# Graph attention kernel, layer 1: the tile's running sum added inside PSUM by an identity matmul and copied back by ScalarE

## What is computed

```python
h = (x @ W).reshape(n, NHEAD, OUT_FEATS)
h_l = (a_l * h).sum(-1)
h_r = (a_r * h).sum(-1)
e = h_l[row] + h_r[col]
e = jnp.where(e > 0, e, ALPHA * e)
m = jax.ops.segment_max(e, row, num_segments=n)
ex = jnp.exp(e - m[row])
denom = jax.ops.segment_sum(ex, row, num_segments=n)
att = ex / (denom[row] + 1e-16)
msg = att[:, :, None] * h[col]
out = jax.ops.segment_sum(msg, row, num_segments=n)
```

## Time and profile before

| | |
|---|---|
| median of 3 runs | 2378.44 us (2374.66 to 2379.36) |
| the profiled execution | 2369.76 us |
| its span (first to last instruction) | 2368.0 us |
| PE busy in the span | 1942.9 us, 82% |
| DVE busy | 1809.6 us, 76% |
| ACT busy | 1484.2 us, 63% |
| POOL busy | 1480.6 us, 63% |
| mean granted clock of PE | 0.939 |

### The profile page before, as it was taken

The page is one execution under the profiler, slowest core; times in us unless marked ns, Lnnn a source line. Parts: engine busy times, 40 slices in busy tenths (PEclk is TensorE's granted clock), DMA queues, the critical chain, the costliest instruction groups (busy, mean ns, idle before and its releaser), DMA issues.

```text
span 2368.0 us, 44546 instructions
## 1 busy us (share of the span) xinstructions
PE 1942.9 (82%) x9766; PEld 1418.9 (60%) x9767; DVE 1809.6 (76%) x4313; ACT 1484.2 (63%) x5321; POOL 1480.6 (63%) x1468
## 2 busy tenths in 40 slices
PE   0889999999938988889898999856777787878774
PEld 0457777777726777777776777633444454545442
DVE  7873333333339998999999999785999998999987
ACT  2236666666637777777777777447666666666660
POOL 3737777777777666666666656137666666666660
PEclk9999999999969999999999999986998988898997
DMA  8343333333339888988888885024344333333311
GB/s 239 123 183 133 131 130 132 131 130 132 122 135 328 292 298 292 299 289 300 301 290 301 303 286 169 3 69 132 102 109 107 107 103 102 107 108 101 107 36 54
DMA packets 162160, 403.34 MB, mean 170 GB/s; under 512 B 46887, under 2 KB 59099, under 8 KB 162108
## 3 DMA queue, kind: packets, MB, share of 16 engines
q0 software_dynamic: 79360, 276.09, 36.1%
q1 hardware_dynamic: 82748, 126.67, 17.0%
HBM read 343.89 MB, written 84.72 MB: 181 GB/s over the span
## 4 chain that ended last, share of the span: by engine, by line
PE 31%; DVE 29%; issue 16%; DMA 9%; POOL 6%; DVEq 4%; ACT 3%; SPq 0%; ACTq 0%; POOLq 0%
PE ps L1449 12%; DMA arena<-sorted_edges 6%; DVE gmx L1291 5%; POOL sorted_edges L573 4%; PE ps L1435 4%; PE ps L1482 3%; PE ps L1485 3%; DVE arena L1323 3%; DVE sc L1134 2%; PE ps L1497 2%; DVE arena L1120 2%; DVE work L1286 2%; DVEq L337 2%; PE ps L1607 2%; DVE arena L1127 2%
## 5 line engine op out<-in xcount | busy, mean ns | idle before, releaser
L642 POOL DMA_INDIRECT arena<-node_row,idxC x464 | 485.5, 1046 | 234.4 <-issue 133.1
L573 POOL DMA_INDIRECT sorted_edges<-work,idxA x416 | 404.9, 973 | 145.8 <-issue 143.1
L1091 DVE TENSOR_TENSOR work<-ps,b_bc 128x512 f32<-128x512 f32 x208 | 143.8, 691 | 322.2 <-PE ps L1449 322.2
L1449 PE MATMUL ps<-w_sb,arena 128*128 128x256 f32 x1664 | 386.7, 386 | 0.0
L1607 PE MATMUL ps<-arena,hq 128*128 128x260 f32 x928 | 281.6, 431 | 91.6 <-DVE work L1286 88.1
L1449 PEld LDWEIGHTS ps<-w_sb,arena 128*128 128x128 f32 x1664 | 307.7, 190 | 71.8 <-issue 33.8
L597 POOL DMA_INDIRECT work<-node_kvx,idxB x232 | 247.0, 1065 | 147.9 <-issue 50.9
L597 POOL DMA_INDIRECT arena<-node_kvx,idxB x232 | 246.0, 1060 | 146.1 <-issue 56.0
L712 ACT ACTIVATE work<-work 128x256 f32<-128x256 f32 x416 | 188.7, 500 | 194.1 <-DVE work L1091 194.0
L1291 DVE TENSOR_REDUCE gmx<-ps 128x4 f32<-128x1024 f32 x232 | 282.8, 1219 | 28.7 <-PE ps L1582 28.6
L1482 PE MATMUL ps<-arena,work 128*128 128x256 f32 x928 | 254.8, 398 | 57.9 <-issue 37.6
(11 more groups left out here) (206 smaller groups left out, 3858.7 us busy)
## 6 DMA issues: line engine op xcount, KB each, us to landing
arena<-sorted_edges SPq DMA_DIRECT2D x232, 260.0 KB, 4.7
work<-sorted_rows SPq DMA_DIRECT2D x58, 256.0 KB, 3.6
arena<-in_edge_attr SPq DMA_DIRECT2D x25, 512.0 KB
node_kvx<-arena SPq DMA_DIRECT2D x24, 384.0 KB, 2.3
arena<-node_row,idxC POOLq DMA_INDIRECT x464, 3.3
sorted_edges<-work,idxA POOLq DMA_INDIRECT x416, 2.4
sorted_edges<-arena SPq DMA_DIRECT2D x25, 260.0 KB
sorted_edges<-arena SPq DMA_DIRECT2D x1, 6240.0 KB
```

Of the source, the lines that this page charges most:

```text
L573: pool.indirect_dma_start(rec_dram[:, :], bass.IndirectOffsetOnAxis(ap=idxA[:, st.slot(8), c:c + 1], axis=0), recA[:, st.slot(8), c, :], N ...
L642: pool.indirect_dma_start(row1_g[:, st.slot(16), j, :], None, row1_dram[:, :], bass.IndirectOffsetOnAxis(ap=idxC[:, batch(st).slot(4), st. ...
L1449: ins = pe.matmul(ps[:, 5 + t, half * H:(half + 1) * H], hidT[:, r, m, half, t * P:(t + 1) * P], w2_sb[:, m, :], start=m == 0, stop=m == 1)
```

## The change

The sum of a tile no longer passes through DVE.

- **PE**: after the two one-hot matmuls of a step (now 15 steps behind, L1616 of the changed kernel), a third f32 matmul, identity times the tile's `acc1`, adds the old sum in the same bank (L1623). It waits for `acc1_done` of the step before, or, in the first step of a batch, for `acc1_scaled`. Its operand's address is a register, so PE now reads the table `gt_i` every eight steps, between the L1601 matmuls and the one-hot matmuls.
- **ACT**: a copy of the bank to `acc1` (L862), 17 steps behind, placed after `indices`, `pen` and `onehT1` and ahead of the copy of `hrT`. It has a table read of its own every eight steps. The one-hot matrices are made four steps later than before; the exponentials stand at the fourth step of a batch, one step earlier.
- **DVE**: the add is gone. The scale by `mscale` stays, once per batch, now behind the maximum (L1299), and waits for `acc1_done` of the step before. Both table reads of a turn stand behind the maximum.
- `msg1` becomes a ring of eight, half of it in `hq` behind the one-hot matrices; a new semaphore `msg1_used` frees its slots and those of `oneh1`. The table gets 32 columns in front where it had 16, and `ended` shares memory with `away`.

```diff
@@ scalar, layer1
+                if st.u % 8 == 0:
+                    act_tiles[17] = tiles16(ACT_ENGINE, st.k, 17, st.u // 8)
+                d = st.back(17)
+                if d.real():
+                    act.wait_ge(s("agg1_ready"), d.n + 1)
+                    act.copy(acc1[:, bass.ds(act_tiles[17][st.u % 8], 1), :].rearrange("p a n -> p (a n)"),
+                             agg1[d.slot(2)]).then_inc(s("acc1_done"), 1)
...
-                if st.real():
-                    act.wait_ge(s("srcC_ready"), b.n + 1)
+                h = st.back(4)
+                if h.real():
+                    act.wait_ge(s("srcC_ready"), batch(h).n + 1)
...
-                e = b.back(3)
-                if g == 0 and e.real():
+                e = b.back(2)
+                if g == 3 and e.real():
@@ vector, layer1
-                    dve.wait_ge(s("agg1_ready"), c.n + 1)
-                    dve.tensor_tensor(acc, acc, agg1[c.slot(2)], ALU.add).then_inc(
-                        s("acc1_done"), 1)
...
+                if st.u % 8 == 0:
+                    tiles[11] = tiles16(DVE, st.k, 11, st.u // 8)
+                c = st.back(11)
+                if c.real() and c.u % BG == 0:
+                    acc, k = tile(acc1, tiles[11][st.u % 8]), batch(c)
+                    dve.wait_ge(s("mscale"), k.n + 1)
+                    if not c.first(1):
+                        dve.wait_ge(s("acc1_done"), c.n)
...
-                    if not m.first(2):
-                        dve.wait_ge(s("agg1_ready"), m.n - 1)
+                    if not m.first(8):
+                        dve.wait_ge(s("msg1_used"), m.n - 7)
@@ tensor, layer1
-                d = st.back(13)
+                if st.u % 8 == 0:
+                    pe_tiles[15] = tiles16(PE, st.k, 15, st.u // 8)
+                d = st.back(15)
...
+                        ins = pe.matmul(agg1[r], oneh1[:, r16, j, :], msg1(d)[:, j, :],
+                                        start=j == 0, stop=False)
+                    ins.then_inc(s("msg1_used"), 1)
+                    if d.u % BG == 0:
+                        pe.wait_ge(s("acc1_scaled"), batch(d).n + 1)
+                    else:
+                        pe.wait_ge(s("acc1_done"), n)
+                    pe.matmul(agg1[r], ident[:, :],
+                              acc1[:, bass.ds(pe_tiles[15][st.u % 8], 1), :].rearrange("p a n -> p (a n)"),
+                              start=False, stop=True).then_inc(s("agg1_ready"), 1)
```

More of the change, by code:

```diff
@@ L38 @@
 AHEAD = 2
+FRONT = 32
 class Step:
@@ L279, in gnn_kernel @@
         away = sb("away", [P, 2, GJ, P])
+        ended = away.rearrange("p r c n -> p (r c n)")[:, 0:NG]
         sc = sb("sc", [P, 2, GJ, NH0])
@@ L330, in tiles_of @@
             _, values = nc.values_load_multi_w_load_instructions(
-                gt_i[0:1, bass.ds(k * 8 + (16 - lag), count)], engines=(eng,), min_val=0, max_val=NT - 1,
+                gt_i[0:1, bass.ds(k * 8 + (FRONT - lag), count)], engines=(eng,), min_val=0, max_val=NT - 1,
                 skip_runtime_bounds_check_because="the table's values are bounded by the minimum with NT - 1")
@@ L337, in tiles16 @@
             _, values = nc.values_load_multi_w_load_instructions(
-                gt_i[0:1, bass.ds(k * 16 + (16 - lag + 8 * half), 8)], engines=(eng,), min_val=0, max_val=NT - 1,
+                gt_i[0:1, bass.ds(k * 16 + (FRONT - lag + 8 * half), 8)], engines=(eng,), min_val=0, max_val=NT - 1,
                 skip_runtime_bounds_check_because="the table's values are bounded by the minimum with NT - 1")
@@ L856, in layer1 @@
                     act.copy(hrT[0:PARTS, pair(c).slot(2), :], trh).then_inc(s("hrT"), 1)
-                if st.real():
-                    act.wait_ge(s("srcC_ready"), b.n + 1)
+                h = st.back(4)
+                if h.real():
+                    act.wait_ge(s("srcC_ready"), batch(h).n + 1)
                     for j in range(GJ):
[L860 to L865, removed]
+                        act.activation(away[:, h.slot(2), j, :], iota1[:, :], ACT.Abs,
+                                       bias=srcC[:, batch(h).slot(4), h.u % BG, j:j + 1], scale=-1.0).then_inc(
+                                           s("away1"), 1)
+                    act.wait_ge(s("away1"), 2 * h.n + 2)
+                    if not h.first(16):
+                        act.wait_ge(s("msg1_used"), h.n - 15)
+                    act.activation(oneh1[:, h.slot(16), :, :], away[:, h.slot(2), :, :], ACT.Relu, bias=1.0,
                                    scale=-1.0).then_inc(s("oneh1"), 1)
@@ L890, in layer1 @@
                     act.activation(mscale[:, r, :], mdiff[:, r, :], ACT.Exp).then_inc(s("mscale"), 1)
-            run(act, NG, 16, 9, layer1)
+            run(act, NG, 16, 17, layer1)
         @block.vector
@@ L1293, in layer1 @@
                                    axis=AX.X).then_inc(s("gmax"), 1)
[L1294 to L1295 removed]
+                if st.u % 8 == 0:
[6 more added lines that the diff above has]
+                        dve.wait_ge(s("acc1_done"), c.n)
+                    dve.tensor_tensor(acc.rearrange("p (h d) -> p h d", d=HE),
+                                      acc.rearrange("p (h d) -> p h d", d=HE),
+                                      mscale[:, k.slot(2), :].unsqueeze(2).to_broadcast([P, NH1, HE]),
+                                      ALU.mult).then_inc(s("acc1_scaled"), 1)
                 e = b.back(1)
@@ L1606, in layer1 @@
                     for j in range(GJ):
[L1607 to L1611, removed]
+                        ins = pe.matmul(agg1[r], oneh1[:, r16, j, :], msg1(d)[:, j, :],
[8 more added lines that the diff above has]
+                              start=False, stop=True).then_inc(s("agg1_ready"), 1)
+            pe_tiles = {}
+            run(pe, NG, 16, 15, layer1)
 def run8(eng, total, body):
```

15 lines of the change are left out of this document (9 added, 6 removed).

## The result

The changed kernel took **2487.01 us** (median of 4 runs, 2483.3 to 2490.24); the kernel before took 2376.55 beside it. The ratio is 1.0463, with a 95% interval of 1.0444 to 1.0481: slower, by 110 us. The prediction had the direction, but 2428 for the time and 2485 for the end of its range.

A forecast was written before the change was run, and what follows sets the result against it. DVE bounds layer 1 before; afterwards a chain through three engines: 2 x 13.2 + 2 x 12.8 = 52.0 a turn, clock 1.2, so 53.2 against 49.74. Over 13.5 turns +47, drain 2: 2428 us, range 2330 to 2485.

The forecast's parts named there:

- The chain through three engines: Layer 1, once per batch: scale, PE's identity product, ACT's copy, next scale; 11.35, or 13.2 us with PE's read.
- DVE's share below 80%: Sign of being right: DVE's busy share in layer 1, 89% before the change, falls below 80%.
- idle times of about 1.9 under "issue" at L1616: Sign of being right: PE's L1616 has 29 such idle times.
- the turns of 52 to 54: Sign of being right: 16 steps of layer 1 take 52 to 54 us between like DVE instructions, 49.74 before.
- Rival 1: Engines overlap and ACT's stream decides: turn of 16 steps 46 us with frictions, 2328 us in all; chance 0.23.
- the clock: PE at 1.2 GHz behind its reads in layer 1: bounds nothing and 4.8 us a turn, a quarter taken, 1.2.
- the second path: DVE's rows, maxima and logits, then ACT's work and the scale: 11.7 us a batch, 12.8 with ACT's read.
- 13.5 turns: Turns of 16 steps counted in layer 1, of 14.5, as first steps have no sum yet: +47 us.
- The drain: End of layer 1, lagging 17 steps and not 13: between 0 and 6 us more, 2 taken.
- Rival 2: Every layer 1 batch with PE's read runs at 1.2 GHz: turn 56.8 us, 2480 us in all; chance 0.15.
- The ring: The ring of eight, with the later one-hots, takes waits away, but none of those on the layer 1 chain.
- The 0.35 for ACT's copy: ACT's copy of 260 columns out of PSUM: 0.35 us, from layer 0's copy of 256 columns, 354 ns.

The follow-up runs named there:

- x1: Changed kernel with ACT's block of index copies, mask and onehT1 moved from ahead of the new copy to the step's end: 2394.28 us, ratio 1.0085.
- x5: Changed kernel with the edits of x1 and x2 together: 2360.68 us, ratio 0.9926 to the kernel before.
- x3: Changed kernel with PE making the one-hot product three times in each batch's first step: 2461.87 us, ratio 1.0375.
- x11: Changed kernel with ACT's copy and PE's identity product always on tile 0, so neither reads its table in layer 1 (computation changed): 2386.43 us, ratio 1.0048.
- x2: Changed kernel with DVE's table reads moved ahead of the scale, in the batch's last step: 2440.33 us, ratio 1.0268.
- x4: Kernel before with only the ring of eight, its shared memory and the moved memset; DVE keeps its adds: 2376.03 us, ratio 0.9987.
- x10: x5 with the exponentials put directly behind ACT's copy of the new sum: 2359.11 us, ratio 0.9932.
- x13: x10 with PE's identity product always reading tile 0, so PE alone reads no table in layer 1 (computation changed): 2353.26 us, ratio 0.9889.
- x7: x5 with PE making the one-hot product twice in a batch's first step: 2363.21 us, ratio 0.9939.

## Why the prediction was right and wrong

**What bounds it: right.** The chain through three engines with the copy behind mask and onehT1 was named, with its rows, and x1 shows it by one edit. DVE's share below 80%, the copy that ends each idle time at L1299, and L1623 waiting for L1299 were all found as described. Not found were the idle times of about 1.9 under "issue" at L1616 (0.6 on the mean, put down to ACT's L880) and the turns of 52 to 54. Rival 1, free overlap, asked for a border shorter by 0.6 a batch. It did not happen. With another order x5 gets a third of the way there: 2361, where that rival had 2328 and the kernel before takes 2377.

**What the turn costs: wrong by 4.8 (58.0 for 53.2).** Two terms of the sum failed: the clock, taken at 1.2 a turn where it cost 3.3, and DVE's table read in the second path, taken at nothing there where it cost most of 2.6. The batches with PE's read, from the end of one scale to the end of the next, against the terms of the sum:

| piece | forecast | 1962.69 to 1976.87 | 1990.92 to 2006.52 |
|---|---|---|---|
| to `hm_ready` (L1275 ends) | 2.14 | 1.94 | 1.94 |
| to the one-hot product (handover, spreading, read) | 2.36 | 2.45 | 2.68 |
| to the end of the next step's identity product | 3.68 | 4.75 | 5.88 |
| ACT, from copy to copy, to the scale's start | 4.61 | 4.61 | 4.67 |
| scale | 0.43 | 0.43 | 0.43 |
| sum | 13.2 | 14.18 | 15.60 |

- ACT's piece, handovers and maxima were right within 0.2. PE's read was too: from `hm_ready` to the product it is 2.45 and 2.68 for 2.36, and in x3, at full clock, 2.66 (L1275 ends at 1928.82, the product starts at 1931.48). The rows' idle times of 0.46 and 0.69 show only what is left after PE has worked off slow scores. From these three, the read itself seems to start when the spreading is let go. Taking it away gave 1.9 in one of the batches, but 0.8 in the other (x11), where slow scores then stand in its place: there the product still starts 1.71 behind `hm_ready` and not 0.54.
- **The clock** was mis-sized: "a quarter of 4.8". Of the product and the step behind it 1.07 and 2.20 are its price, 3.3 a turn where I had 1.2; x3 gives 3.1. In the turns of 54.8 this piece takes 3.76 (1826.81 to 1830.57), close to the 3.68 forecast. I set its chance by layer 0's seven slow groups of 27, whose idle time is the read's 1.9. Here PE had idled 3.8 ahead of the identity product, the sum of all lateness on the circle, and I had estimated "1 to 2". The idle time is much the same in the turns of 54.8 (3.8 to 3.9); what differs is whether the clock is back before the product, 4 us later.
- **The second path missed DVE's own read.** I priced both reads in DVE's stream, at 0.72 each, and not in the path over the logits, where the first maximum of a batch is followed after 2.19 and not 1.13. 1.06 of it, and 0.34 at 1950.87 for PE's late scores, make 14.17 and 14.05 out of 12.8: 2.6 a turn. x2 took it away, and those batches took 13.1.

These are all of it: 52.0 + 3.3 + 2.6 and 0.1 left over make 58.0.

**How often.** I multiplied one price by 13.5 turns. Eight turns cost 8.3 each, 66; what is left of the 94.6 are 28 for the other five or so, which ran at 53.1 to 58.7, most at 55 and 56. One price for all would have given 112.

**The drain** was 6.9, where I took 2 and bounded it at 6: the last copies wait one by one for PE.

**Rival 2** gave the number (2480 for 2487), and by the sign set for it, L1616 over 1.5 in most groups (some 20 of the 28 behind the read), it is the case that came. Its number is half luck: its clock was 1.5 a turn too dear (4.8 for 3.3), which hid a part of the missing 2.6 of DVE's read; and it took every turn at that price. The ring "takes waits away, but none of these": right (x4). The 0.35 for ACT's copy was 0.37 by the groups, 373 ns for 167 of them; the 403 ns estimated from the Trainium skill (ScalarE: Activation LUTs, What ACT_TABLE_LOAD costs) was further off, and neither matters.

**Left open.** The split of x11's gain between the two engines' reads and the clock is read from the lengths of its batches; neither read was taken away by itself in the changed kernel. That x10 holds at two paths of equal length is read from x13's waits alone; ACT's read by itself was not taken away there. And the 9 us or so ahead of layer 1 have no cause here.

## What to carry to other kernels

When a running value is handed around several in-order engines, ask of every engine what stands ahead of its handover, not how busy it is: one block of 2.3 us ahead of a 0.37 us copy cost 93 us here, and moving it and one engine's reads turned 4.6% slower into 0.7% faster. Put each table read into *every* path that crosses it, not only into the stream of its engine, and measure it from the event that lets it go, since an idle time in a row shows only what other work didn't cover. Where the slack of a circle piles up in one place on PE, add all of it before you judge the clock.

## What the runs showed of the hardware

- Adding matmuls shortened the program: three one-hot products for one at a batch's start (1.76 us more a batch) kept the granted clock at 0.98 where it was 0.87, and the time fell by 25 us (x3). With the clock at 0.99 already, two products for one gave nothing (x7).
- In the changed kernel PE idle for 3.7 to 3.9 us was followed by the identity product at 1.23, idle for 0.8 to 1.8 (x1 and x3 too) by one at 0.70. In between the same wait went both ways: 2.97 and 2.98 in the changed kernel by 1.23 and 0.70, and 2.6 in x11 by 1.24 or 0.70, about as often. How long the lower clock then lasted varied in one execution, behind the same wait of 3.9: the product 4 us later took 1.14 or 2.10, and the turn 54.8 or 58.0.
- A table read on PE shows as 0.46 to 0.69 of idle time behind slow work and as 2.0 to 2.1 behind fast work, with the same 2.4 to 2.7 from the end of L1275, which releases the spreading, to the product (the change and x3).
